# Nucleus search of a four-layer graph kernel: two guessed points per row on ScalarE instead of three fixed ones, one more turn of pipeline depth, and one VectorE trial fewer in the second step

## The reference, cut to what matters

```python
def _adj_from_feats(Xa, W1, W2, W3):
    Q = Xa @ W1
    K = Xa @ W3
    logits = Q @ W2 @ K.T / TAU
    idx = jnp.argsort(-logits, axis=1)
    vals = jnp.take_along_axis(logits, idx, axis=1)
    csum = jnp.cumsum(jax.nn.softmax(vals, axis=1), axis=1)
    k_i = jnp.sum(csum < P_NUC, axis=1) + 1
    ...
    masked = jnp.where(keep, logits, -jnp.inf)
    return jax.nn.softmax(masked, axis=1)
for s in range(STEPS):                      # STEPS = 2
    A = _adj_from_feats(Xa, W1, W2, W3)
    Xf = Rf @ Xf
    Xb = Rb @ Xb
    Xa = A @ Xa
    Z = Z + (Xf @ U1[s] + Xb @ U2[s] + Xa @ U3[s])
```

## Time and profile before

| what | value |
|---|---|
| three runs | 3638.29, 3640.17, 3642.70 us |
| profiled execution, first to last instruction | 3639.0 us (no other time is given for it; it lies inside the runs) |
| TensorE busy | 3175.4 us, 87% |
| VectorE busy | 2635.1 us, 72% |
| ScalarE busy | 1889.6 us, 52% |
| GpSimd busy | 996.2 us, 27% |
| trials on VectorE, 208 of them | 778.0 us |
| turns of the loop, 81 of them, MAX8 and MATCH_REPLACE8 | 293.8 and 293.1 us |
| ScalarE's sums over fixed points, 312 of them | 479.6 and 479.1 us |
| mean granted TensorE clock | 0.941 |

### The profile page before, as it was taken

The page is one execution under the profiler, slowest core; times in us unless marked ns, Lnnn a source line. Parts: engine busy times, 40 slices in busy tenths (PEclk is TensorE's granted clock), DMA queues, the critical chain, the costliest instruction groups (busy, mean ns, idle before and its releaser), DMA issues. The chain is left out here.

```text
span 3639.0 us, 40362 instructions
## 1 busy us (share of the span) xinstructions
PE 3175.4 (87%) x13212; PEld 2289.6 (63%) x13212; DVE 2635.1 (72%) x3794; ACT 1889.6 (52%) x2355; POOL 996.2 (27%) x2293
## 2 busy tenths in 40 slices
PE   4999899987999999999875878667899889996799
PEld 3788688875677776777633445344555555554688
DVE  6963400006999999999839999999999999998100
ACT  2211311218788787888744556545565556563100
POOL 1212411211122221212211334334434334334211
PEclk9999999988999999999987989888999999998899
DMA  6544444432122221212221111111122222222255
GB/s 251 209 156 137 129 154 162 160 119 64 51 67 61 55 69 56 67 56 56 58 82 39 51 48 44 45 40 49 51 80 63 68 78 58 76 81 75 69 196 179
DMA packets 142416, 328.49 MB, mean 90 GB/s; under 512 B 15457, under 2 KB 95393, under 8 KB 130977
## 3 DMA queue, kind: packets, MB, share of 16 engines
q1 hardware_dynamic: 142240, 326.31, 28.3%
HBM read 287.59 MB, written 38.67 MB: 90 GB/s over the span
## 5 line engine op out<-in xcount | busy, mean ns | idle before, releaser
L1345 DVE SCALAR_TENSOR_TENSOR U<-E,trial 128x3327 f32<-128x3327 f32 x208 | 778.0, 3740 | 0.0
L880 PE MATMUL bank<-Hc,PT 128*128 128x256 f32 x2704 | 647.0, 392 | 68.8 <-ACT PT L1062 68.8
L880 PEld LDWEIGHTS bank<-Hc,PT 128*128 128x128 f32 x2704 | 528.0, 197 | 194.4 <-ACT PT L1062 92.3
L920 PE MATMUL bank<-big,adj 128*128 128x512 f32 x1352 | 613.7, 605 | 0.0
L1022 ACT ACTIVATE junk<-E,neg_3c 128x3327 uint8<-128x3327 f32 x156 | 479.1, 3071 | 5.1
L1022 ACT ACTIVATE junk<-E,neg_c 128x3327 uint8<-128x3327 f32 x156 | 479.6, 3074 | 1.7
L920 PEld LDWEIGHTS bank<-big,adj 128*128 128x128 f32 x1352 | 254.9, 194 | 329.4 <-issue 327.6
L893 PE MATMUL tr<-ident,E 128*128 128x128 f32 x1352 | 200.3, 291 | 275.5 <-DVE E L1394 275.5
L1062 ACT ACTIVATE PT<-tr 128x1024 f32<-128x1024 f32 x208 | 176.9, 851 | 369.2 <-PE tr L893 369.2
L893 PEld LDWEIGHTS tr<-ident,E 128*128 128x128 f32 x1352 | 172.8, 151 | 305.9 <-DVE E L1394 287.4
L920 PE MATMUL bank<-Hc,adj 128*128 128x256 f32 x1352 | 319.1, 388 | 0.0
(11 more groups left out here) (231 smaller groups left out, 4481.7 us busy)
## 6 DMA issues: line engine op xcount, KB each, us to landing
adj<-adjT SPq DMA_DIRECT2D x131, 448.0 KB, 3.4
E<-adjT SPq DMA_DIRECT2D x32, 1664.0 KB, 7.0
adj<-adjT SPq DMA_DIRECT2D x104, 384.0 KB, 3.4
adj<-adjT SPq DMA_DIRECT2D x20, 1664.0 KB, 7.0
adj<-adjT SPq DMA_DIRECT2D x14, 1216.0 KB, 5.7
E<-adjT SPq DMA_DIRECT2D x13, 1216.0 KB, 5.8
xt<-xin SPq DMA_DIRECT2D x52, 128.0 KB, 5.8
x_d<-xn SPq DMA_DIRECT2D x52, 128.0 KB, 1.7
```

Source lines behind the costliest of these rows:

```text
L880: last = mm(axp[:, 0:D], PT[k % 2][:, h, i * P:(i + 1) * P], Hc[:, j], start=(k == 0 and h == 0 and i == 0), stop=(k == SLOTS - 1 and h == ...
L920: last = mm(agg[:, 0:w], adj[:, j], rhs[:, j], start=(j == 0), stop=False)
L1345: V_.scalar_tensor_tensor(out=U[:, 0:N], in0=e, scalar=point, in1=e, op0=ALU.is_ge, op1=ALU.mult, accum_out=found))
```

## The change

- ScalarE's six passes over fixed points become four over two points that are worked out per row: Relu and Sign at a first guess, then Relu and Sign at a second.
- GpSimd's `bracket` is replaced by `guess` (first point from the row's mean score, maximum and sum), `update(t, 0)` (second point from the sums at the first) and `update(t, 1)` (end of the bracket and first trial point from the sums at the second). The order of GpSimd's round changes: its adds first, then `guess`, then `update(t-1, 1)`, layer-norm steps, `update(t, 0)`.
- `EVALS` goes from (3, 5) to (3, 4).
- A fourth score buffer; search, turn and post move one round later (`LAG` 4 to 5, `LATE` 5 to 7), so there are 64 rounds instead of 62.
- To make room, `K2` is halved, and the adjacency tile has two parts of seven blocks instead of four parts: a chunk is loaded when the one two before it has been used. SyncE's stores move between the loads of the next round.
- ScalarE's copies of the scores also give their sum. The mass above the upper end comes from the closing pass instead of being carried along.

The diff, cut to its core:

```diff
-EVALS = (3, 5)
-MAX_AFTER = (1, 2)
-AIM = 3.0
-KEEP_END = 0.8
-FIXED = (0.008, 0.03, 0.1)
+EVALS = (3, 4)
+PASSES = (2, 2)
+POINTS = 2
+SHIFT = (1.4, 0.0)
+STEER = (2.0, 4.0)
+AIM = (3.0, 4.0)
+KEEP_END = (0.8, 0.75)
+RIDGE = (8.0, 4.0)
-LAG = 4
-LATE = 5
+DEPTH = 4
+LAG = 5
+LATE = 7
+SPAN = 7
-        E = sb("E", [P, 3, NP])
+        E = sb("E", [P, DEPTH, NP])
-        K2 = sb("K2", [P, NP])
+        K2 = sb("K2", [P, NP // 2])
-        xz = sb("xz", [P, 2, D])
+        xz = adj[:, 22:26].rearrange("p (a j) q -> p a (j q)", a=2)
-            PT = [ab(f"PT{k}", [P, 2, max(WIDE[k::2]) * P]) for k in range(2)]
+            PT = [adj[:, 14:22].rearrange("p (h j) q -> p h (j q)", h=2), ab("PT1", [P, 2, max(WIDE[1::2]) * P])]
-            search_at = lambda i: shown(i - 2)
-            turn_at = lambda i: shown(i - 3)
-            post_at = lambda i: shown(i - 4)
+            aim_at = lambda i: shown(i - 2)
+            search_at = lambda i: shown(i - 3)
+            turn_at = lambda i: shown(i - 4)
+            post_at = lambda i: shown(i - 5)
...
                         def load_chunk(n, k):
                             j0, j1 = AGG[k], AGG[k + 1]
-                            sp.dma_start(adj[:, j0:j1], adjT[n % NT, :, j0:j1]).then_inc(adj_in[k], 16)
+                            to = SPAN * (k % 2)
+                            sp.dma_start(adj[:, to:to + j1 - j0], adjT[n % NT, :, j0:j1]).then_inc(adj_in[k], 16)
...
+                            for k in range(SLOTS):
+                                if n is not None:
+                                    sp.wait_ge(agg_part, SLOTS * n + k + 1)
+                                    if k < 2:
+                                        load_chunk(n, k + 2)
...
+                                    elif n + 1 < tiles:
+                                        load_chunk(n + 1, k - 2)
+                                if k == 0 and i >= 1:
+                                    store(i - 1)
...
+                        def sums(t, j, m):
+                            if m == 0:
+                                act.wait_ge(aimed[j], t + 1)
...
+                            func, acc_ = ((ACT.Relu, over), (ACT.Sign, sign))[m]
+                            go(junk[:, 0:N], E[:, t % DEPTH, 0:N], func, bias=negp[:, t % 2, j:j + 1], scale=1.0,
+                               accum_out=acc_[:, t % 2, j:j + 1]).then_inc(summed[j], 1)
                                 if k == 0 and F is not None:
...
-                                    fixed(F, 0, 2)
+                                if k == 0 and R is not None:
+                                    sums(R, 1, 0)
+                                if k == 3 and F is not None:
+                                    sums(F, 0, 1)
-                                    if F is not None:
-                                        fixed(F, 2, 4)
+                                    if R is not None:
+                                        sums(R, 1, 1)
                                     if F is not None:
-                                        fixed(F, 4, 2 * NF)
+                                        sums(F, 0, 0)
...
+                        def offer(t, j):
+                            then(ts(negp[:, t % 2, j:j + 1], cand[:, t % 2, 0:1], -UNDER, None, ALU.mult))
+                            pool.sem_inc(aimed[j], 1)
+
+                        def prepare(t):
...
+                            then(ts(up[:, q, 0:2], known[:, 4 + 2 * step:6 + 2 * step], p, ga[:, q, 12:13], ALU.mult, ALU.add),
+                                 ts(up[:, q, 3:4], p, p, RIDGE[step] ** 2, ALU.mult, ALU.mult))
+                            then(tt(up[:, q, 4:5], up[:, q, 3:4], ga[:, q, 11:12], ALU.mult))
+
+                        def guess(t):
...
+                            pool.wait_ge(exp_done, t + 1)
...
+                            then(tt(ga[:, q, 0:2], musum[:, q, 0:2], musum[:, q, 2:4], ALU.add),
+                                 tt(ga_(2), z, root, ALU.pow))
+                            then(tt(ga_(3), ga_(0), ga_(1), ALU.add),
+                                 ts(ga_(4), ga_(2), ROOT, -ROOT - math.log(N), ALU.mult, ALU.add))
+                            then(ts(ga_(5), ga_(3), 1.0 / N, nm, ALU.mult, ALU.add))
+                            then(tt(ga_(6), ga_(4), ga_(5), ALU.subtract))
+                            then(ts(ga_(7), ga_(6), 2.0, 0.01, ALU.mult, ALU.add),
+                                 ts(ga_(8), ga_(5), 1.0, -SHIFT[step], ALU.mult, ALU.add))
+                            then(tt(ga_(9), ga_(7), half, ALU.pow),
+                                 tt(ga_(10), ga_(8), ga_(7), ALU.add))
+                            then(ts(ga_(13), ga_(9), -QUANTILE, ga_(10), ALU.mult, ALU.add))
+                            then(ts(ga_(14), ga_(13), -0.001, -36.0, ALU.min, ALU.max))
+                            then(tt(p, e_, ga_(14), ALU.pow))
+                            offer(t, 0)
+                            then(tt(shape4(parts[:, 0]), z.to_broadcast([P, 4]), shape4(outset[:, 0]), ALU.mult),
+                                 ts(tgt, z, P_NUC, None, ALU.mult),
+                                 ts(ga_(12), z, -P_NUC, None, ALU.mult),
+                                 tt(ga_(15), z, minus, ALU.pow))
+                            then(tt(ends2[:, d], parts[:, 0], outset[:, 1], ALU.add),
+                                 ts(below, tgt, 1 - 2.0 ** -24, None, ALU.mult),
+                                 ts(ga_(11), ga_(15), ga_(9), 1.0 / DENSITY, ALU.mult, ALU.mult))
+                            prepare(t)
+
+                        def update(t, j):
...
+                            pool.wait_ge(summed[j], PASSES[j] * (t + 1))
+                            then(ts(count, sign[:, q, j:j + 1], 0.5, N / 2, ALU.mult, ALU.add))
+                            then(ts(mass_, count, p, over[:, q, j:j + 1], ALU.mult, ALU.add))
+                            then(ts(cand[:, q, 1:3], up[:, q, 0:2], mass_, None, ALU.add),
+                                 ts(took[:, 1:2], mass_, tgt, None, ALU.is_ge))
+                            if j > 0:
+                                then(tt(up_(16), mass_, up_(7 + j), ALU.subtract))
+                                then(ts(up_(17), up_(16), up_(16), up_(3), ALU.mult, ALU.add),
+                                     tt(up_(18), up_(16), up_(20), ALU.mult))
+                                then(tt(up_(19), up_(17), minus, ALU.pow),
+                                     tt(up_(18), up_(4), up_(18), ALU.subtract))
+                                then(tt(slope, up_(18), up_(19), ALU.mult))
+                            then(tt(up_(21), slip, slope, ALU.mult),
+                                 ts(took[:, 0:3:2], took[:, 1:2].to_broadcast([P, 2]), -1.0, 1.0, ALU.mult, ALU.add))
...
+                            then(ts(up_(20), up_(21), STRIDE, -STRIDE, ALU.min, ALU.max),
+                                 tt(parts[:, 0], ends, wide(took[:, 0:2]), ALU.mult),
+                                 tt(parts[:, 1], cand[:, q, 0:2].unsqueeze(1).to_broadcast([P, 2, 2]),
+                                    wide(took[:, 1:3]), ALU.mult))
+                            then(tt(up_(22), e_, up_(20), ALU.pow),
+                                 tt(ends, parts[:, 0], parts[:, 1], ALU.add))
+                            then(tt(up_(23), up_(22), p, ALU.mult))
+                            if j < POINTS - 1:
+                                then(ts(p, up_(23), hi, lo, ALU.min, ALU.max))
+                                offer(t, j + 1)
+                                prepare(t)
+                            else:
+                                then(ts(point, up_(23), hi, lo, ALU.min, ALU.max))
+                                pool.sem_inc(bracketed, 1)
...
-                            then(V_.tensor_copy(mass[:, 0:1], hi[:, 2:3]),
-                                 V_.memset(E[:, t % 3, N:NP], 0.0),
+                            then(V_.memset(E[:, t % DEPTH, N:NP], 0.0),
                                  V_.scalar_tensor_tensor(out=U[:, 0:N], in0=e, scalar=hi[:, 0:1], in1=e,
-                                                         op0=ALU.is_ge, op1=ALU.subtract, reverse1=True))
+                                                         op0=ALU.is_lt, op1=ALU.mult, accum_out=sc[:, 5:6]))
+                            then(V_.tensor_tensor(mass[:, 0:1], Zs[:, q:q + 1], sc[:, 5:6], ALU.subtract))
```

More of the change, by code:

```diff
@@ L718, in build @@
             last_at = lambda i: post_at(i - 2) - NT if second(post_at(i - 2)) else None
-            rounds = NT + LAG + NT + 6
+            rounds = NT + LAG + NT + 7
             early = NT - LAG
-            spread = [b for i in range(rounds + 1) for b in [last_at(i)] if b is not None and i <= tiles + LATE]
+            spread = [b for i in range(rounds + 1) for b in [last_at(i)] if b is not None and i < tiles + LATE]
             kept = len(spread)
@@ L756, in build @@
                 max_ready, exp_done, probs_ready = s("max_ready"), s("exp_done"), s("probs_ready")
```

(18 more changed lines are left out.)

395 lines of the change are left out of this document (180 added, 215 removed).

## The result

The changed kernel takes 3488.2 us (median of 4 runs, 3486.7 to 3489.1) against 3640.9 us for the kernel before on the same chip: ratio 0.958, interval 0.9566 to 0.9593, 152.7 us less. The forecast was 3578 us, 62 us less, in a range from 3475 to 3700. The sign was right and the time lay in the range, near its lower end; the gain was 2.5 times the forecast.

What follows compares the result with a forecast made beforehand. Before the change TensorE was taken to bound step 0 and VectorE step 1; afterwards GpSimd, locked out by VectorE's passes, decides. Start +21, step 0 +33, gap +12, step 1 -128 make -62: 3578 us, range 3475 to 3700.

Steps and rivals of the forecast that it cites:

- The lock and GpSimd's round: GpSimd stands still during VectorE's passes over two SBUF tensors; its round takes 39.4 us in step 0, 49.6 in step 1.
- Step 0: First attention step: 24 rounds at GpSimd's 39.4 us and two shorter ones, 1012 us against 978, +33.
- The gap: Between the steps, where VectorE's search stands still for 68.7 us: 12 us more, bounds 0 and 30.
- The start: The round added at the start costs 21 us, bounds 15 and 30.
- Step 1: Second attention step: one trial fewer, 46 turns, one-turn tiles mostly at GpSimd's 49.6 us: 1343 us against 1471, -128.
- The extra turn: Search one round later: VectorE's wait for the bracket, 43.3 us in all, goes; two rounds are added.
- The sum: Whole kernel: 21 + 33 + 12 - 128 = -62 us, giving 3578 us.
- A: Rival: GpSimd keeps pace, step 0 at TensorE's 36.94 us a tile, step 1 -168; 3479 us, chance 0.20.
- B: Rival: two-scalar tensor_scalar takes 0.1 us more, GpSimd's round grows 3.1 us, +118; 3696 us, chance 0.16.
- C: Rival: the search ends wider, 66 turns in step 1, only -18 there; 3688 us, chance 0.09.
- D: Rival: step 1 still needs 51 turns, only the removed trial is bought; 3609 us, chance 0.55 together with the forecast.
- The half tile of adjacency: SyncE's chunk loads into the two-part adjacency tile cost nothing; if the cover is gone, at most 177 us.

Runs made afterwards that it cites:

- e2: The kernel after with ten more chained 128x1 products on GpSimd ahead of each guess, results unused: 3583.9 us.
- e4: As e3, and each trial's pass over two tensors is a plain sum over one tensor of the same length: 3298.7 us.
- e6: The kernel after with turns fixed: one per tile in step 0; in step 1 one in even and three in odd tiles: 3506.9 us.
- e3: The kernel after with exactly one turn of the MAX8 loop in every tile: 3444.1 us.
- e1: The kernel before with EVALS = (3, 4), one trial fewer in step 1 and nothing else: 3832.4 us, ratio 1.0529.
- e7: The kernel after without the extra turn of depth (LAG 4, LATE 5), four score buffers kept: 4458.9 us.
- e12: The kernel after with GpSimd's seven 128x256 operations per tile of step 1 made on one column alone: 3457.3 us.

## Why the prediction was right and where it was wrong

*The lock and GpSimd's round: right.* 49.6 us were forecast for step 1 and 48.8 measured, 39.4 and 38.8 for step 0. The work was 28.4 (28.0 forecast) and 21.8 (21.4), the standing still 20.4 (21.6) and 16.9 (18.0): the prediction took 3.6 us a pass, but an operation that is held does its own work in that time too. e2 and e4 move the time, e2 by GpSimd's work and e4 by the lock.

*Step 0: right in mechanism, 11 us too dear.* +22.0 against +33: the round was overrated by 0.6 us, 14 us in 24 rounds. *The gap:* +11.8 against +12. It was a choice between 0 and 30, and no run takes the gap apart, so that it met the number may be luck.

*The start: too dear.* +5.6 against +21. The first row maxima of the kernel after:

```profile
818.56 3.62 DVE L1361 TENSOR_REDUCE nmax<-E 128x1 f32<-128x3327 f32 x1 [21.49 <-ACT E L1070]
838.47 3.62 DVE L1361 TENSOR_REDUCE nmax<-E 128x1 f32<-128x3327 f32 x1 [16.28 <-ACT E L1070]
859.27 3.62 DVE L1361 TENSOR_REDUCE nmax<-E 128x1 f32<-128x3327 f32 x1 [17.19 <-ACT E L1070]
```

The added round does take 20 to 21 us, as forecast. But the old interval of 30.2 us, which the prediction left as it was, is gone: two intervals of together 40.7 us stand in its place, and the first maximum comes 3.3 us earlier. The prediction laid the 30.2 us to a cold clock and six passes; the clock granted in them was 0.94 (822 to 852 us), so little of it was the clock.

*Step 1: the failed step.* It was forecast at 1343 us and took 1281.5, 62 us less. The prediction wrote "9 x 49.6 + 42.1 + 13 x 51.5 + ...", the larger of GpSimd's and VectorE's time for each tile by itself, 75 us above VectorE alone (1268). Of the 75, the nine tiles at 49.6 in place of 42.1 are 67.5; the rest is mostly that two-turn tiles stand at 51.5, not at 42.1 + 8.8 = 50.9, which the prediction doesn't explain. Measured are 31 us above VectorE alone, so 44 of the 62 come from here. The extra turn and the fourth buffer carry a lead over (e6 shows the trading; which of the two carries it, no run tells apart): after a tile of 60 us GpSimd is ahead and the next tile's bracket, exponential and scores are there, as e6 shows with 40.2 us tiles and no wait. The prediction allowed the two-turn tiles of step 0 to "fit into the extra buffer's slack" and didn't carry the same thought into step 1. The waits that did come, 24.6 us, stand where five one-turn tiles follow each other (the 10th to the 14th) and in the tile behind them, when the lead is used up; with one turn everywhere (e3) they stand in each from the seventh on, but for the last two. The other 18 us are one turn less (45, not 46, 9 us) and VectorE's tiles, 40.1 us where nothing collides and 42.3 in the second half, where I took 42.1 throughout. The prediction also miscounted the old step 1: its nine, twelve, three and two tiles make 50 turns, and the trace has eight with one turn and thirteen with two; the sum doesn't use them.

*The sum:* 62 in step 1, 15 at the start, 11 in step 0, 2 in the rest: the 90 us between -62 and -152. All four misses go the same way, so they add up and none hides another.

*The rivals.* A's time (3479) came nearest, but not by its mechanism: GpSimd doesn't keep pace in step 0, whose 26 us of gain never came. B's price per operation wasn't there: the work came out 0.4 us above the forecast, not 3.1. C (66 turns) wasn't either; e1 shows how large that risk was: 90 turns for the same four trials with the fixed points. D's reading, that the new points buy little, is the opposite of what e1 suggests. The half tile of adjacency cost next to nothing, as forecast: TensorE waits 5.5 us in all for loads of `adj` in the attention part, in the 13 rounds with layer 3's products.

*The extra turn* was priced by the 43 us wait of the kernel before. That wait is indeed gone, but it says nothing of what the turn carries once the chain is longer: 971 us (e7).

## What to carry to other kernels

Where two engines work on the same tiles and there is a buffer or a turn between them, compare their means over as many tiles as the lead can last, not the larger of the two for each tile; take the larger only where the short tiles follow each other. Then look for a third engine that is nearly full in part of the stretch, as TensorE is in the second half of step 1: it caps what either of the two can win. A change that makes a chain longer and gives it a turn of depth has to be priced with both, since neither means anything alone. And an operation moved to an idle engine goes where that engine waits anyway: the same add went with 26 us at the end of layer 1's chain and cost nothing in a gap.

## What I had not expected of the hardware

The standing still is mutual. GpSimd's operations that begin within a pass of VectorE over two tensors end with it or just behind (up to 4.25 us for a 0.73 us add), and GpSimd's 128x256 adds hold up VectorE: small operations of 0.16 us take 0.4 to 0.7 us, passes of 3.7 us take 4.2, 47 us of VectorE's time in all (e12). A trial over one tensor leaves GpSimd free: the same 4214 instructions are busy for 1528.6 us in place of 2202.6 (e4, e3). So in e3 some 30% of GpSimd's busy time is standing still in the trials alone, and a busy share has to be read with that in mind.
